# Four transfers instead of one for the reload of the residual, with a signal each, in a four-layer transformer kernel

## The chip, the cores and the metric

The kernel runs on one core of a Trainium2 chip, as one launch. The metric is the device time of that core in microseconds, the median of several runs; lower is better. In the traces PE is TensorE (matmuls and transposes), PEld its weight loads, DVE VectorE, ACT ScalarE, POOL GpSimd and SP SyncE, which in this kernel only issues transfers between memory and SBUF.

## The reference, cut to what matters

The input x has shape (32, 64, 256), that is N = 2048 rows of D = 256 numbers, and goes through four layers, each of a "cond" part and an "ffn" part, with a residual sum around each layer:

```
x = x + L0_ffn(L0_cond(x, cond), ...)      # ffn: mixture of 8 experts, top 2, capacity 320 rows per expert
x = x + L1_ffn(L1_cond(x, cond), ...)      # cond: 4 gated experts and a shared one
x = x + L2_ffn(L2_cond(x, ...), ...)       # ffn: 8 experts, each takes its 512 best rows
x = x + L3_ffn(L3_cond(x, cond, ...), ...) # cond: norm, attention, MLP in hyperbolic form
```

The ffn parts of layers 0 and 2 scatter-add their experts' outputs to rows of the result. L3_cond begins with a layer norm over the 256 numbers of each row:

```
m = x.mean(-1); v = ((x - m) ** 2).mean(-1)
xn = layer_norm(logmap0(x));  xm = expmap0(xn * (1 + sc_msa) + sh_msa);  q = plin(xm, w_q, b_q); ...
```

## The kernel before, in words

The residual lives in SBUF as `st.res`, 128 partitions x 16 tiles x 256 numbers (2 MB); tile t holds rows 128 t to 128 t + 127. The 2048 rows are also spoken of as four blocks of 512 rows, NB = 4, four tiles (TPB = 4) each. `st.cT` is the same data turned, with the 256 numbers in two groups (KC = 2) on the partitions and the rows along the free axis.

The program is a row of phases. Each phase opens a `Block`, in which every engine gets its own instruction list; at the end of a block all engines meet, and only then does the next phase begin. At the end of a layer `layer_end` (lines 59 to 75) adds one more block, in which GpSimd clears the layer's semaphores; semaphores made by `of_pool_dma` are not cleared.

The expert phase `routed_moe_phase` (lines 529 to 730) runs twice, as e0 at the end of layer 0 and as e3 at the end of layer 2. Before it, the dispatch phase has written the residual to the DRAM tensor `token_sums` (`sums` in the code, line 449). In the phase, GpSimd gathers each expert's rows, TensorE multiplies, VectorE scales the results (line 700), and GpSimd adds them to `token_sums` by indirect transfers (line 597), counted in `y_out`. When all are in, SP brings `token_sums` back into `st.res` in one transfer (line 575) and waits for it (line 576).

What follows differs:

- After e0 come `layer_end` and `turn_phase` "t1" (lines 128 to 155): for c in 0, 1 and b in 0 to 3 TensorE turns four tiles (line 138), group g = 4c + b; VectorE copies the even groups (line 145) and ScalarE the odd ones (line 153) from PSUM to `st.cT`. Then the block ends, and l1_cond begins with SP's weight transfers (line 1119), of which the first writes into `st.res` again.
- After e3 come `layer_end` and `l3_cond` (from line 2189). The work of its engines follows an order written out by hand in `l3_order()`. It begins with the statistics of tiles 0 to 7 (line 2617), then the norm's lengths, logarithm and variance for these eight tiles together (lines 2622 to 2648), and `norm` of tiles 0 to 7 (`stretch` at line 2655, then line 2667). Tiles 0 to 3 use the first chunk of the modulation `mod`, tiles 4 to 7 the second. TensorE turns tiles 0 and 1 after norms 2 and 3 (line 2328); its first product with `w_qkv` (line 2342) waits for three weight and three bias transfers at once (`qkv_in` of 96). The result is read by line 2682, which also needs the norm's last factor (lines 1906 to 1908). Statistics of tiles 8 to 15 come in the middle of this first round.
- SP in `l3_cond` issues, in this order: modulation chunks 0 and 1 (two transfers of 512 KB each, line 2273), then w_q, b_q, w_k, b_k, w_v, b_v (lines 2286 and 2289), then chunk 2 once four norms are done, chunk 3 once eight are, and then w_o, gates, w_f1, w_f2 and the rest.

`turn_phase` runs once more, as "t0" at the start of the program, with its rows loaded by the setup phase, which waits for them.

Of the kernel before, what the change touches and what calls it, by code (L numbers as in the profile page):

```python
# [14 lines left out]
P = 128  # L15
# [71 lines left out]
def setup_phase(nc, sem, st, x, cond):  # L87

    loaded, const0, const1 = sem("setup_loaded"), sem("setup_const0"), sem("setup_const1")
    turned, kept = sem("setup_turned"), sem("setup_kept")  # L90
    with nc.sbuf_tensor("cond_rows", [B, D], F32) as cond_rows, \
            nc.psum_tensor("cond_ps", [P, KC, B], F32) as cond_ps, nc.Block() as block:

        @block.sync
        def _(sp):
            sp.dma_start(cond_rows[:, :], cond).then_inc(loaded, 16)
            sp.dma_start(st.res[:, :, :], x.rearrange("(t a) s d -> (a s) t d", a=2)).then_inc(st.res_loaded, 16)
            sp.wait_ge(st.res_loaded, 16)

        @block.gpsimd  # L100
        def _(pool):
            pool.memset(st.ident[:, :], 0.0).then_inc(const0, 1)
            pool.memset(st.tri[:, :], 1.0).then_inc(const0, 1)
            pool.memset(st.ones[:, :], 1.0).then_inc(const0, 1)
            pool.wait_ge(const0, 3)
            pool.affine_select(out=st.ident[:, :], in_=st.ident[:, :], compare_op=ALU.not_equal, fill=1.0,
                               base=0, pattern=[[-1, P]], channel_multiplier=1).then_inc(const1, 1)

            pool.affine_select(out=st.tri[:, :], in_=st.tri[:, :], compare_op=ALU.is_ge, fill=0.0,
                               base=0, pattern=[[1, P]], channel_multiplier=-1).then_inc(const1, 1)  # L110

        @block.tensor
        def _(pe):
            pe.wait_ge(loaded, 16)
            pe.wait_ge(const1, 2)
            for c in range(KC):
                last = pe.transpose(cond_ps[:, c, :], cond_rows[:, c * P:(c + 1) * P], st.ident[0:B, 0:B])
            last.then_inc(turned, 1)

        @block.vector  # L120
        def _(dve):
            dve.wait_ge(turned, 1)
            dve.tensor_copy(st.condT[:, :, :], cond_ps[:, :, :]).then_inc(kept, 1)
            dve.wait_ge(kept, 1)

def turn_phase(nc, sem, st, tag, src, dst):

    turned, kept = sem(tag + "_turned"), sem(tag + "_kept")  # L130
    with nc.psum_tensor(tag + "_ps", [P, 8, 4, P], F32) as ps, nc.Block() as block:

        @block.tensor
        def _(pe):
            for g in range(KC * NB):
                c, b = g // NB, g % NB
                for j in range(TPB):
                    last = pe.transpose(ps[:, g, j, :], src[:, b * TPB + j, c * P:(c + 1) * P], st.ident[:, :])
                last.then_inc(turned, 1)

        @block.vector
        def _(dve):
            for g in range(0, KC * NB, 2):
                dve.wait_ge(turned, g + 1)
                dve.tensor_copy(dst[:, g // NB, (g % NB) * BLK:(g % NB + 1) * BLK],
                                ps[:, g, :, :].rearrange("p a b -> p (a b)")).then_inc(kept, 1)
            dve.wait_ge(kept, KC * NB)

        @block.scalar
        def _(act):  # L150
            for g in range(1, KC * NB, 2):
                act.wait_ge(turned, g + 1)
                act.activation(dst[:, g // NB, (g % NB) * BLK:(g % NB + 1) * BLK],
                               ps[:, g, :, :].rearrange("p a b -> p (a b)"), ACT.Copy).then_inc(kept, 1)
            act.wait_ge(kept, KC * NB)
# [370 lines left out]
            link(dve.tensor_tensor(st.slot_row[:, :, :], got[:, :, :, 1], row[:, :, :], ALU.add))  # L526


def routed_moe_phase(nc, sem, st, tag, rows, sums, slots, W1, b1, W2, func, spares, later_weights=None):

    tiles = [(a, min(P, slots - a)) for a in range(0, slots, P)]
    J = len(tiles)
    names = ("b_in b_turned b_kept w1_hi w2_hi w1_split w2_split x_turned x_hi x_ready up_done act_done h_ready "
             "y_done scaled res_in").split()
    b_in, b_turned, b_kept, w1_hi, w2_hi, w1_split, w2_split, x_turned, x_hi, x_ready, up_done, act_done, h_ready, \
        y_done, scaled, res_in = (sem(f"{tag}_{x}") for x in names)
    w1_in, w2_in = ([sem(f"{tag}_{x}_in{i}") for i in range(2)] for x in ("w1", "w2"))
    y_out = sem.of_pool_dma(tag + "_y_out")
    gathered = [sem.of_pool_dma(f"{tag}_gathered{i}") for i in range(3 * J)]
# [1 line left out]
    with ExitStack() as mem:  # L541
# [17 lines left out]
        @block.sync  # L559
        def _(sp):  # L560
            for e in range(E8):
                if e >= 2:
                    sp.wait_ge(w1_split, 2 * (e - 1))
                sp.dma_start(w1_raw[e % 2], W1[e].rearrange("(c p) f -> p c f", p=P)).then_inc(w1_in[e % 2], 16)
                if e == 0:
                    sp.dma_start(st.b1rows[:, :], b1.rearrange("e (c p) -> (e c) p", p=P)).then_inc(b_in, 16)
                if e >= 2:
                    sp.wait_ge(w2_split, 2 * (e - 1))
                sp.dma_start(w2_raw[e % 2], W2[e].rearrange("(c p) d -> p c d", p=P)).then_inc(w2_in[e % 2], 16)
                if e == 1 and rounding:  # L570
                    rounding.load(sp)
            if rounding:
                rounding.store(sp)
            sp.wait_ge(y_out, 16 * E8 * J)
            sp.dma_start(st.res[:, :, :], sums[0:N, :].rearrange("(t p) d -> p t d", p=P)).then_inc(res_in, 16)
            sp.wait_ge(res_in, 16)

        @block.gpsimd
        def _(pool):
# [1606 lines left out]
    yield from moved(range(NT + HALF, 2 * NT), False)  # L2186


def l3_cond(nc, sem, st, x, dst, w, ada_rows):

    QKV_PARTS = lambda t: [(0, 512), (512, 768)] if t < HALF else [(0, 256), (256, 512), (512, 768)]
    qkv_before = lambda t: 2 * t if t <= HALF else 2 * HALF + 3 * (t - HALF)
# [4 lines left out]
    with ExitStack() as mem:  # L2197
# [412 lines left out]
        def _(dve):  # L2610
            link = Chain(dve, chain)
            mean, var = mv[:, :, 0], mv[:, :, 1]

            def stats(m):
                if m >= NT:
                    dve.wait_ge(moved, m - NT + 1)
                dve.bn_stats(six[:, m % NT, :], (x if m < NT else dst)[:, m % NT, :]).then_inc(stats_done, 1)
# [459 lines left out]
def adaln_ffn_4_layers(nc, a, out):  # L3077

    with ExitStack() as stack:
        sem = Sems(nc)  # L3080
        st = State(nc, stack, sem)
        w = lambda prefix, *names: [a[prefix + n] for n in names]
        spare = st.cT2[:, :, :].rearrange("p c (t d) -> p (c t) d", d=D)
        rows = nc.dram_tensor("token_rows", (N + PADS, ROW), F32).ap()
        sums = nc.dram_tensor("token_sums", (N + PADS, D), F32).ap()

        ada_rows = nc.dram_tensor("modulation_rows", (B, ADA), F32).ap()
        kept_gu = nc.dram_tensor("rounded_gate_up", (P, GT * D), F32).ap()
        kept_dn = nc.dram_tensor("rounded_down", (P, KC * HID), F32).ap()

        setup_phase(nc, sem, st, a["x"], a["cond_1024"])

        turn_phase(nc, sem, st, "t0", st.res, st.cT)
        l0_cond_phase(nc, sem, st, st.cT, st.cT2, *w("L0_cond_", "W_q", "b_q", "W_kv", "b_kv", "no_op_k", "no_op_v", "W_proj", "b_proj"))
        l0_router_phase(nc, sem, st, st.cT2, *w("L0_ffn_", "router_w", "router_b"),
                        *w("L3_cond_", "w_ada", "b_ada"), ada_rows)
        bias2_phase(nc, sem, st, "b20", st.gates, st.res, *w("L0_ffn_", "b2"))
        dispatch_phase(nc, sem, st, "d0", st.cT2, rows, sums)
        routed_moe_phase(nc, sem, st, "e0", rows, sums, CAPACITY, *w("L0_ffn_", "w1", "b1", "w2"), ACT.Gelu, [st.cT, st.cT2],
                         [*w("L3_ffn_", "w_gate", "w_up", "w_down"), kept_gu, kept_dn])  # L3100
        sem.layer_end()

        turn_phase(nc, sem, st, "t1", st.res, st.cT)
        l1_phases(nc, sem, st, a)
        sem.layer_end()

        l2_cond_phase(nc, sem, st, st.cT, st.cT2, *w("L2_cond_", "Wx", "Wh", "b"))
        l2_router_phase(nc, sem, st, st.cT2, *w("L2_ffn_", "Wr"))
        bias2_phase(nc, sem, st, "b23", st.gates, st.res, *w("L2_ffn_", "b2"), accT=st.cT)
        dispatch_phase(nc, sem, st, "d2", st.cT2, rows, sums)  # L3110
        routed_moe_phase(nc, sem, st, "e3", rows, sums, CHOSEN, *w("L2_ffn_", "W1", "b1", "W2"), ACT.Gelu, [st.cT, st.cT2])
        sem.layer_end()

        names = "w_q b_q w_k b_k w_v b_v w_o b_o w_f1 b_f1 w_f2 b_f2".split()
        l3_cond(nc, sem, st, st.res, spare, dict(zip(names, w("L3_cond_", *names))), ada_rows)
        sem.layer_end()
        l3_ffn_phases(nc, sem, st, spare, st.res, out, kept_gu, kept_dn)
        sem.stack.close()
        sem.kept.close()
# [18 lines left out]
```

## Time and profile before

| | |
|---|---|
| median of 3 runs | 2501.59 us (2500.58 to 2502.45) |
| the profiled execution's own time | 2501.92 us |
| its span in the profile | 2500.2 us |
| granted TensorE clock, mean over the span | 0.892 |
| busy: PE, DVE, ACT, POOL | 84%, 54%, 39%, 10% |
| moved by transfers | 146.01 MB, 58 GB/s over the span |

The page cuts the span in 40 slices of 62.5 us; most of them show PE at 8 or 9 tenths. The reloads lie at 298.4 us (fifth slice) and 1839.5 us (thirtieth slice). In both slices PE is less busy than in those before them.

### The profile page before, as it was taken

The numbers are of one execution on the slowest core, as the hardware profiler recorded it, in microseconds if no ns is written. First come the engines' busy times: TensorE is split into PE (matmuls) and PEld (weight loads), VectorE is DVE, ScalarE is ACT, GpSimd is POOL, SyncE is SP. The second block draws the span as 40 slices with busy tenths as digits, with TensorE's granted clock in tenths as the row PEclk, the third lists the DMA queues.
The fourth block names the chain that finished last, engine by engine and source line by source line (L and its number), as shares of the span: only waits on it lengthen the run. The fifth ranks groups of instructions, "written<-read, shape, count | busy, mean of one in ns | idle before, by whom it ended". The sixth has DMA issues, their size and how long they took to land. (4 is left out here: it accounts for less than half of the span.)

```text
span 2500.2 us, 34348 instructions
## 1 busy us (share of the span) xinstructions
PE 2107.1 (84%) x13371; PEld 1693.4 (68%) x13371; DVE 1353.5 (54%) x2579; ACT 985.5 (39%) x1954; POOL 244.1 (10%) x207
## 2 busy tenths in 40 slices
PE   6788689999799999999999883789946777785786
PEld 5477668888687888888888673479934554554554
DVE  2589555777575444444343214456546446454885
ACT  2143255555253444444444220235423344454222
POOL 1144200000000000000000002047710000000000
PEclk7799889999899999999999995689976857897998
DMA  2375221233113121111100000265363001000000
GB/s 77 99 230 159 61 69 58 79 102 101 35 34 78 42 51 34 27 42 34 34 1 1 11 3 0 86 193 131 67 145 93 2 18 34 18 18 35 1 9 26
DMA packets 111492, 146.01 MB, mean 58 GB/s; under 512 B 6661, under 2 KB 94660, under 8 KB 111077
## 3 DMA queue, kind: packets, MB, share of 16 engines
q1 hardware_dynamic: 101220, 129.99, 17.3%
q0 software_dynamic: 10112, 13.85, 3.1%
q8 instruction: 106, 1.74, 0.3%
q14 instruction: 54, 0.43, 0.1%
HBM read 121.83 MB, written 21.99 MB: 58 GB/s over the span
## 5 line engine op out<-in xcount | busy, mean ns | idle before, releaser
L1598 DVE TENSOR_TENSOR m_h_lo<-m_hf,m_h_hi 128x512 fp32r<-128x512 f32 x256 | 172.1, 690 | 359.1 <-ACT m_hf L1573 357.2
L1570 ACT ACTIVATE m_h_hi<-m_h_ps,m_bT 128x512 fp32r<-128x512 f32 x256 | 177.0, 691 | 367.6 <-PE m_h_ps L394 348.0
L1573 ACT ACTIVATE m_hf<-m_h_ps,m_bT 128x512 f32<-128x512 f32 x256 | 175.0, 684 | 0.0
L597 POOL DMA_INDIRECT token_sums<-e_y,slot_row x56 | 145.7, 2602 | 159.4 <-DVE e_y L700 147.2
L662 ACT ACTIVATE e_h_hi<-e_h_ps,e_b1T 128x320 fp32r<-128x320 f32 (+1 forms) x128 | 78.0, 609 | 168.3 <-PE e_h_ps L394 102.2
L1310 DVE TENSOR_TENSOR c_h_lo<-c_hf,c_h_hi 128x512 fp32r<-128x512 f32 x120 | 82.3, 687 | 74.8 <-ACT c_hf L1269 73.7
L716 DVE TENSOR_TENSOR e_h_lo<-e_hf,e_h_hi 128x320 fp32r<-128x320 f32 (+1 forms) x128 | 74.1, 589 | 77.5 <-issue 44.4
L1837 POOL MEMSET n_bias<- 128x256 f32 x1 | 0.3, 312 | 1083.5 <-POOLq L59 1083.5
L1266 ACT ACTIVATE c_h_hi<-c_h_ps,c_b 128x512 fp32r<-128x512 f32 x88 | 62.2, 707 | 109.3 <-PE c_h_ps L394 108.8
L394 PE MATMUL m_y_ps<-m_h_hi,l_w_1hi 128*128 128x512 f32 x256 | 100.3, 392 | 3.5 <-issue 3.5
L394 PE MATMUL m_h_ps<-m_x_hi,l_w_0hi 128*128 128x512 f32 x256 | 100.6, 393 | 0.4 <-ACT m_b2T L1563 0.4
L394 PE MATMUL m_y_ps<-m_h_hi,l_w_0hi 128*128 128x512 f32 x256 | 99.7, 389 | 1.4 <-ACT m_gT L1584 1.4
L394 PE MATMUL m_y_ps<-m_h_hi,l_w_1lo 128*128 128x512 f32 x256 | 100.3, 392 | 0.0
L394 PE MATMUL m_h_ps<-m_x_hi,l_w_0lo 128*128 128x512 f32 x256 | 100.3, 392 | 0.0
L394 PE MATMUL m_h_ps<-m_x_lo,l_w_0hi 128*128 128x512 f32 x256 | 100.3, 392 | 0.0
L394 PE MATMUL m_y_ps<-m_h_lo,l_w_1hi 128*128 128x512 f32 x256 | 100.2, 391 | 0.0
L394 PE MATMUL m_y_ps<-m_h_hi,l_w_0lo 128*128 128x512 f32 x256 | 99.6, 389 | 0.0
L394 PE MATMUL m_y_ps<-m_h_lo,l_w_0hi 128*128 128x512 f32 x256 | 99.6, 389 | 0.0
L394 PE MATMUL m_h_ps<-m_x_hi,l_w_1hi 128*128 128x512 f32 x256 | 99.6, 389 | 0.0
L394 PE MATMUL m_h_ps<-m_x_lo,l_w_1hi 128*128 128x512 f32 x256 | 99.6, 389 | 0.0
L394 PE MATMUL m_h_ps<-m_x_hi,l_w_1lo 128*128 128x512 f32 x256 | 99.6, 389 | 0.0
L2342 PE MATMUL l_ps<-l_w_qkv,l_qkv_T 128*128 128x256 f32 (+1 forms) x160 | 64.7, 548 | 28.5 <-ACT l_qkv_T L2493 19.2
(644 smaller groups left out, 5607.7 us busy)
## 6 DMA issues: line engine op xcount, KB each, us to landing
cT<-in_L_ffn_W_dram SPq DMA_DIRECT2D x30, 1024.0 KB, 5.3
res<-in_L_cond_ew_dram SPq DMA_DIRECT2D x22, 1024.0 KB, 5.3
cT<-in_L_ffn_w_dram SPq DMA_DIRECT2D x16, 1024.0 KB, 7.0
res<-gates_rows SPq DMA_DIRECT2D x8, 1024.0 KB, 15.0
l_mod<-modulation_rows SPq DMA_DIRECT2D x16, 512.0 KB, 6.6
token_rows<-d_tok SPq DMA_DIRECT2D x2, 2112.0 KB, 9.9
token_sums<-res SPq DMA_DIRECT2D x2, 2048.0 KB, 7.6
res<-token_sums SPq DMA_DIRECT2D x2, 2048.0 KB, 8.4
```

The costliest lines, as they stand in the source:

```text
L394: ins = pe.matmul(out, lhs[a], rhs[b], start=(first and i == 0), stop=(last and i == 2))
L597: pool.indirect_dma_start(out=sums, out_offset=bass.IndirectOffsetOnAxis(ap=st.slot_row[0:r, e, j:j + 1], axis=0), in_=y[0:r, e % 2, j, :] ...
L662: act.activation(hs[0][:, f, :], h_ps[:, f % HB, 0:slots], func, bias=b1T[:, n:n + 1])
L716: dve.tensor_tensor(hs[1][:, f, :], hf[:, f % HB, :], hs[0][:, f, :].bitcast(F32), ALU.subtract).then_inc(h_ready, 1)
L1266: act.activation(hs[0][:, f, :], h_ps[:, f % HB, :], ACT.Gelu_apprx_tanh, bias=b[:, f:f + 1])
L1310: dve.tensor_tensor(hs[1][:, f, :], hf[:, f % HB, :], hs[0][:, f, :].bitcast(F32), ALU.subtract).then_inc(h_ready, 1)
L1570: act.activation(hs[0][:, f, :], h_ps[:, f % HB, :], ACT.Relu, bias=bT[:, at:at + 1])
L1573: act.activation(hf[:, f % HB, :], h_ps[:, f % HB, :], ACT.Relu, bias=bT[:, at:at + 1]).then_inc(act_done, 1)
L1598: dve.tensor_tensor(hs[1][:, f, :], hf[:, f % HB, :], hs[0][:, f, :].bitcast(F32), ALU.subtract).then_inc(h_ready, 1)
L1837: pool.memset(bias[:, :], 0.0).then_inc(bias_set, 1)
L2342: last = pe.matmul(ps[:, qkv_bank(t, p), 0:z - a], qkv_T[:, t % 2, k, :], w_qkv[:, k, a:z], start=(k == 0), stop=(k == KC - 1))
```

## The change

- Line 575's one transfer of 2 MB becomes four of 512 KB, one for each block of 512 rows. Each has a semaphore of its own, four for the first reload and four for the second. The wait at line 576 goes.
- The semaphores are made by `of_pool_dma`, so `layer_end` does not clear them.
- `turn_phase` takes the list of semaphores: TensorE waits for block b's ahead of the four transposes of (c = 0, b). For "t0" none are given, and it stays as it was.
- In `l3_cond` VectorE waits for block m/4's semaphore ahead of the statistics of tiles 0, 4, 8 and 12. All later readers of `st.res` there come behind the statistics.

```
-def turn_phase(nc, sem, st, tag, src, dst):
+def turn_phase(nc, sem, st, tag, src, dst, src_in=None):
...
             for g in range(KC * NB):
                 c, b = g // NB, g % NB
+                if src_in is not None and c == 0:
+                    pe.wait_ge(src_in[b], 16)
                 for j in range(TPB):
...
             sp.wait_ge(y_out, 16 * E8 * J)
-            sp.dma_start(st.res[:, :, :], sums[0:N, :].rearrange("(t p) d -> p t d", p=P)).then_inc(res_in, 16)
-            sp.wait_ge(res_in, 16)
+            for b in range(NB):
+                sp.dma_start(st.res[:, b * TPB:(b + 1) * TPB, :],
+                             sums[b * BLK:(b + 1) * BLK, :].rearrange("(t p) d -> p t d", p=P)).then_inc(res_in[b], 16)
...
             def stats(m):
+                if m < NT and m % TPB == 0:
+                    dve.wait_ge(x_in[m // TPB], 16)
                 if m >= NT:
                     dve.wait_ge(moved, m - NT + 1)
...
+        res_in = [[sem.of_pool_dma(f"res_in{i}_{b}") for b in range(NB)] for i in range(2)]
...
-        turn_phase(nc, sem, st, "t1", st.res, st.cT)
+        turn_phase(nc, sem, st, "t1", st.res, st.cT, res_in[0])
...
-        l3_cond(nc, sem, st, st.res, spare, dict(zip(names, w("L3_cond_", *names))), ada_rows)
+        l3_cond(nc, sem, st, st.res, res_in[1], spare, dict(zip(names, w("L3_cond_", *names))), ada_rows)
```

## Rows read from the trace of the kernel before

**Rows 1.** The page: the 40 slices of PE busy and of granted clock.

```profile
PE   6788689999799999999999883789946777785786
...
PEclk7799889999899999999999995689976857897998
```

**Rows 2.** Timeline, first reload: start, length (us), engine, line, out<-in, [idle before <-releaser].

```profile
298.40 0.37 SPq L575 DMA_DIRECT2D res<-token_sums  x1
...
308.16 5.23 PE L138 MATMUL t_ps<-ident,res 128*128 128x128 f32 x32 [18.00 <-PEq L59]
309.28 0.69 DVE L145 COPY cT<-t_ps 128x512 f32<-128x512 f32 x1 [17.82 <-PE t_ps L138]
310.13 0.60 ACT L153 ACTIVATE cT<-t_ps 128x512 f32<-128x512 f32 x1 [27.47 <-PE t_ps L138]
...
312.99 0.69 DVE L145 COPY cT<-t_ps 128x512 f32<-128x512 f32 x1 [0.18 <-PE t_ps L138]
313.43 0.60 ACT L153 ACTIVATE cT<-t_ps 128x512 f32<-128x512 f32 x1 [0.28 <-PE t_ps L138]
314.48 0.38 SPq L1119 DMA_DIRECT2D res<-in_L_cond_sw_dram  x1
```

**Rows 3.** Transfers by line: count, KB each, median us from issue to landing.

```profile
cT<-in_L_ffn_W_dram SPq DMA_DIRECT2D x30, 1024.0 KB, 5.3
...
res<-token_sums SPq DMA_DIRECT2D x2, 2048.0 KB, 8.4
...
l_wkv<-in_L_cond_W_kv_dram SPq DMA_DIRECT2D x1, 512.0 KB, 3.8
```

**Rows 4.** Windows, first reload: PE, PEld, DVE, ACT, POOL, clock, DMA share, GB/s.

```profile
305.00:306.00 1.00, 0.00 (x0) 0.00 (x0) 0.00 (x0) 0.00 (x0) 0.00 (x0) 0.50 0.98 308
306.00:307.00 1.00, 0.00 (x0) 0.00 (x0) 0.00 (x0) 0.00 (x0) 0.00 (x0) 0.50 0.09 29
...
308.10:311.40 3.30, 3.24 (x16) 3.27 (x17) 1.10 (x2) 0.60 (x1) 0.00 (x0) 0.51 0.00 0
311.40:314.50 3.10, 1.99 (x18) 1.75 (x16) 1.67 (x3) 1.80 (x4) 0.01 (x1) 1.00 0.00 0
```

**Rows 5.** Timeline, second reload and start of l3_cond.

```profile
1839.49 0.37 SPq L575 DMA_DIRECT2D res<-token_sums  x1
1848.87 2.62 SPq L2273 DMA_DIRECT2D l_mod<-modulation_rows  x4
...
1848.92 2.71 DVE L2617 BATCH_NORM_STATS2 l_six<-res 128x6 f32<-128x256 f32 x8 [18.36 <-PEq L59]
...
1857.82 0.88 DVE L2655 SCALAR_TENSOR_TENSOR l_xn<-res,l_mv,l_mod 128x256 f32<-128x256 f32 x2
...
1861.68 0.48 DVE L2655 SCALAR_TENSOR_TENSOR l_xn<-res,l_mv,l_mod 128x256 f32<-128x256 f32 x1 [0.62 <-DMA l_mod<-modulation_rows]
...
1864.42 4.51 PE L2342 MATMUL l_ps<-l_w_qkv,l_qkv_T 128*128 128x512 f32 x8 [3.60 <-DMA l_b_qkv<-in_L_cond_b_v_dram]
...
1867.17 0.17 DVE L1908 SCALAR_TENSOR_TENSOR l_fac<-l_nv,l_fac 128x8 f32<-128x8 f32 x1
...
1868.20 1.25 DVE L2682 SCALAR_TENSOR_TENSOR l_wide<-l_ps,l_fac,l_b_qkv 128x512 f32<-128x512 f32 x2 [0.86 <-PE l_ps L2342]
```

**Rows 6.** Windows, second reload and start of l3_cond, columns as in rows 4.

```profile
1847.00:1848.00 1.00, 0.00 (x0) 0.00 (x0) 0.00 (x0) 0.00 (x0) 0.00 (x0) 0.50 0.09 31
...
1850.00:1851.00 1.00, 0.00 (x0) 0.00 (x0) 1.00 (x5) 0.17 (x1) 0.00 (x0) 0.50 0.57 182
...
1856.00:1857.00 1.00, 0.00 (x0) 0.00 (x0) 0.66 (x4) 0.20 (x1) 0.00 (x0) 0.50 1.07 211
...
1862.00:1863.00 1.00, 0.00 (x0) 0.00 (x0) 0.90 (x3) 0.40 (x2) 0.00 (x0) 0.50 1.07 377
```

**Rows 7.** Timeline, SP in l3_cond: a short issue and one held up.

```profile
1855.25 0.47 SPq L2289 DMA_DIRECT2D l_b_qkv<-in_L_cond_b_v_dram  x1
...
1873.65 7.34 SPq L2289 DMA_DIRECT2D l_b_f<-in_L_cond_b_f_dram  x1
```

More of the change, by code:

```diff
@@ L526, in _, with routed_moe_phase @@
             link(dve.tensor_tensor(st.slot_row[:, :, :], got[:, :, :, 1], row[:, :, :], ALU.add))
-def routed_moe_phase(nc, sem, st, tag, rows, sums, slots, W1, b1, W2, func, spares, later_weights=None):
+def routed_moe_phase(nc, sem, st, tag, rows, sums, slots, W1, b1, W2, func, spares, res_in, later_weights=None):
     tiles = [(a, min(P, slots - a)) for a in range(0, slots, P)]
@@ L533, in routed_moe_phase @@
     names = ("b_in b_turned b_kept w1_hi w2_hi w1_split w2_split x_turned x_hi x_ready up_done act_done h_ready "
-             "y_done scaled res_in").split()
+             "y_done scaled").split()
     b_in, b_turned, b_kept, w1_hi, w2_hi, w1_split, w2_split, x_turned, x_hi, x_ready, up_done, act_done, h_ready, \
-        y_done, scaled, res_in = (sem(f"{tag}_{x}") for x in names)
+        y_done, scaled = (sem(f"{tag}_{x}") for x in names)
     w1_in, w2_in = ([sem(f"{tag}_{x}_in{i}") for i in range(2)] for x in ("w1", "w2"))
@@ L2186, in l3_order, with l3_cond @@
     yield from moved(range(NT + HALF, 2 * NT), False)
-def l3_cond(nc, sem, st, x, dst, w, ada_rows):
+def l3_cond(nc, sem, st, x, x_in, dst, w, ada_rows):
     QKV_PARTS = lambda t: [(0, 512), (512, 768)] if t < HALF else [(0, 256), (256, 512), (512, 768)]
@@ L3098, in adaln_ffn_4_layers @@
         dispatch_phase(nc, sem, st, "d0", st.cT2, rows, sums)
-        routed_moe_phase(nc, sem, st, "e0", rows, sums, CAPACITY, *w("L0_ffn_", "w1", "b1", "w2"), ACT.Gelu, [st.cT, st.cT2],
+        routed_moe_phase(nc, sem, st, "e0", rows, sums, CAPACITY, *w("L0_ffn_", "w1", "b1", "w2"), ACT.Gelu, [st.cT, st.cT2], res_in[0],
                          [*w("L3_ffn_", "w_gate", "w_up", "w_down"), kept_gu, kept_dn])
         sem.layer_end()
-        turn_phase(nc, sem, st, "t1", st.res, st.cT)
+        turn_phase(nc, sem, st, "t1", st.res, st.cT, res_in[0])
         l1_phases(nc, sem, st, a)
@@ L3110, in adaln_ffn_4_layers @@
         dispatch_phase(nc, sem, st, "d2", st.cT2, rows, sums)
-        routed_moe_phase(nc, sem, st, "e3", rows, sums, CHOSEN, *w("L2_ffn_", "W1", "b1", "W2"), ACT.Gelu, [st.cT, st.cT2])
+        routed_moe_phase(nc, sem, st, "e3", rows, sums, CHOSEN, *w("L2_ffn_", "W1", "b1", "W2"), ACT.Gelu, [st.cT, st.cT2], res_in[1])
         sem.layer_end()
         names = "w_q b_q w_k b_k w_v b_v w_o b_o w_f1 b_f1 w_f2 b_f2".split()
-        l3_cond(nc, sem, st, st.res, spare, dict(zip(names, w("L3_cond_", *names))), ada_rows)
+        l3_cond(nc, sem, st, st.res, res_in[1], spare, dict(zip(names, w("L3_cond_", *names))), ada_rows)
         sem.layer_end()
```

## The prediction

> **What bounds the kernel now.** I read the page first [rows 1]: TensorE is busy at 8 or 9 tenths through most of the span, so a change away from it is worth nothing except where it stands idle. The two slices with the reloads are such places. The timelines and windows around them show how long nobody works. At the first [rows 2, 4] SP issues at 298.40, the transfer takes 8.4 us [rows 3], so it lands at 306.80, and TensorE's first transpose is at 308.16: 1.36 us for SP to leave its block, the semaphore block and the entry of the next. The data had stopped moving shortly after 306.0 (DMA share 0.98, then 0.09). The 32 transposes take 5.23 us, with the copies right behind, and the next phase starts at 314.48. At the second [rows 5, 6] the issue is at 1839.49, the landing by the same 8.4 at 1847.89, and the next phase starts at 1848.87. All engines are idle until then. So both reloads lie whole on the path that sets the end, and any microsecond saved there is saved at the end, unless a later wait takes it.
>
> **The first reload, step by step.** SP now issues four transfers. The short issues of this queue take 0.37 to 0.47 us [rows 2, 7] and four issues in a row took 2.62 us [rows 5], so SP is done 1.5 to 2.6 us after 298.40. It then goes through the block ends, about 1.36 us, and TensorE stands in front of its first wait at 301.3 to 302.4. When does block 0 land? 512 KB took 3.8 us, 1 MB 5.3 and 2 MB 8.4 [rows 3]: about 3.0 us per MB more and a start of some 2.3. One after another on one queue without gaps they land at about 302.2, 303.7, 305.3 and 306.8. The block ends are then hidden under the first transfer; without that cover they would cost their 1.36 us again. For the three extra completions I add 0.2 us, bounds 0 (the long window of rows 6 shows no gap between transfers) and 1.0: last landing 307.0.
>
> TensorE turns blocks 0 to 2 of c = 0 meanwhile. After the last landing remain 4 transposes of block 3 and 16 of c = 1, five groups of four. A group takes 0.85 us at the low clock (309.28 to 310.13) and 0.44 at the high one (312.99 to 313.43) [rows 2]; the granted clock was 0.51 until 311.4 and 1.00 after [rows 4], 1.2 and 2.4 GHz. In the kernel before, it rose after 3.3 us of unbroken transposes. Afterwards TensorE works in pieces of 0.85 us with 0.7 us of idleness between them until 307, so the clock may be up at once (five groups 2.2 us) or never within this phase (4.25). I take 3.5: like before, about 3.3 us low and then high. PE ends at 307.0 + 0.1 + 3.5 = 310.6, the last ScalarE copy and the block's end add the same 1.09 us as now (313.39 to 314.48), and the next phase starts at 311.7 instead of 314.5. **Gain 2.8 us**; bounds 1.0 (clock low throughout, 1.0 us of extra completions) and 4.3 (clock high at once, none).
>
> The Trainium skill, "TensorE: Matmul & The Clock Gate", Part 4: PE-mode transpose, says that transposes do not bring the clock up. By that rule the five groups would take 4.25 us and the gain would be 2.0; the trace speaks against it, since the clock rose to 1.00 with nothing but transposes running [rows 4].
>
> The four waits in TensorE's list stand only in c = 0; queued behind each are the later groups, and VectorE and ScalarE wait for those. The copies, 0.69 and 0.60 us each on two engines [rows 2], keep step and have done c = 0's first three before the end, so they stay one copy behind. l1_cond's weight transfer into st.res comes behind the block's end, as now; it and everything after move along with it.
>
> **The second reload.** Here two chains run. VectorE's: statistics of tiles 0 to 7 need only blocks 0 and 1, which land at about 1843.3 and 1844.8. Each four take 1.36 us (2.71 for eight), so they end at 1846.2 instead of 1851.63 [rows 5]: 5.4 us earlier. The statistics of tiles 8 to 15 wait for blocks that have landed 20 us before, at no cost. But the norms also need the modulation and TensorE the weights, and those come on the same queue behind the residual. Now tile 4's stretch at 1861.68 waits for chunk 1 of the modulation, and the first product at 1864.42 for the last bias. Between 1850.4 and that landing the transfer engines are full (share 0.57, then 1.07) [rows 6]. What can be gained there is the pause in which they carry nothing: the residual's data end at 1847.1 (0.09), the modulation's begin at 1850.4 (0.57 of the slice). SP would issue the modulation from 1839.49 + 2.0 + 1.0 = 1842.5 on, well ahead of 1847.1, so the queue goes straight on and everything behind arrives 3.3 us earlier: chunk 1 at 1858.4, the bias at 1861.1. The chain behind chunk 1 (to the factor at 1867.34) and the one behind the bias (to 1868.20) end within 0.9 us of each other and move equally. Less 0.2 for the completions and 0.1 for hand-over: **gain 3.0 us**. Upper bound 5.4 (VectorE's whole lead), lower bound 0. Most of VectorE's lead turns into a wait for chunk 0, then for chunk 1.
>
> **Sum.** 2.8 + 3.0 = 5.8 us. The profiled execution took 2501.92 us (span 2500.2), the median is 2501.59, 0.3 lower. 2501.9 - 5.8 = 2496.1 for such an execution, 2495.8 for the median. Elsewhere nothing is touched: four more waits in TensorE's and VectorE's lists and six more issues on SP, all counted above.
>
> **The rivals.**
> - **The queue or SP holds the modulation back.** A later bias issue took 7.34 us instead of 0.47 [rows 7], so SP can be stopped while many transfers are pending. With 2 MB pending and four chunks behind them it could be stopped here; if the modulation's data then begin one start (1.5 us, from issue at 1848.87 to data at 1850.4) after the residual's end, the second gain is 3.3 - 1.5 = 1.8 less 0.3, and with the low clock at the first reload (2.0) the sum is 3.5: 2498.1. For it: the held issue. Against: ten transfers in a row were issued here without such a stop. 21%.
> - **The block's end waits for SP's own transfers.** Then removing line 576 does nothing but shorten SP's last step, and the start is as late as now: 0 to 1 us of gain, 2501.1. Nothing in the trace shows a block left with a transfer pending, so it is open. 6%.
> - **The modulation is not queued behind the residual but shares the engines with it, and VectorE's chain sets the end.** Its lead of 5.4 us survives: 2.8 + 5.4 = 8.2, time 2493.4. Against: the share of 1.07 has no room for more. 7%.
> - **Slower: four transfers are served one by one, each with its own start.** Place: the queue between 298.4 and the last landing, and the same at the second. Four times 3.8 is 15.2 instead of 8.4 us, the last landing 6.8 later. First reload: 313.6 + 0.1 + 3.5 + 1.1 = 318.3, 3.8 us later; second: the modulation's data begin at 1853.9 (6.8 after 1847.1) instead of 1850.4, 3.5 later: sum 7.3, time 2508.9. It decides once the extra starts delay the last landing by over 2.9 us, about 1 us each. Against: ten transfers of 128 to 512 KB in a row kept the share at 1.0 [rows 5, 6]. 5%.
>
> The Trainium skill, "DMA: Bandwidth & Descriptors", Bandwidth, advises transfers of at least 1 MiB and speaks against cutting 2 MB in four. Its price is that of the last rival if nothing overlaps; rows 6 show small ones overlapping.
>
> **How the numbers follow.** The forecast has 61%. Its own range is 2493.9 to 2498.6: the two gains at (4.3, 3.4) and (1.0, 2.0). About a tenth of a percent, 2.5 us, is one free choice of the clock's rise at the two places; executions also scatter by 1 us. The whole range, 2493.2 to 2499.6, takes in the third rival and most of the first and leaves out the second, the slow one and some tails. 0.2%, about what a measurement of this kernel can tell from no change, is 5.0 us, so 2496.6. The forecast falls on the faster side in four of five cases: 0.49 + 0.07 = 0.56. Same: 0.12 + 0.21 + 0.06 = 0.39. Slower: 0.05.
>
> **What would show it.** Right: four issues of SP, landings about 1.5 us apart, the last within 0.5 of the old one; the turning's first transposes before the last landing; the phase start at line 1119 some 13.3 us after the issue instead of 16.1; no empty slice between the residual's and the modulation's data; line 2682 first at some 25.7 us after the issue instead of 28.7. Wrong: TensorE's first transpose after the last landing (second rival), landings 3 us apart or more (slow rival), a gap in the transfers with a long SP issue (first rival). If all these hold and the time is still off by over 2 us, a wait further down took the gain, most likely a clock that fell or rose elsewhere.

## The result, and the profile after

| | before | changed |
|---|---|---|
| median of 10 runs each | 2500.85 us (2497.80 to 2506.03) | 2492.35 us (2490.34 to 2495.29) |
| ratio, 95% interval | | 0.9967 [0.9958, 0.9976] |
| profiled execution, its span | 2501.92, 2500.2 us | 2495.29, 2493.6 us |
| mean granted clock of the profiled execution | 0.892 | 0.889 |

The changed kernel is 8.5 us faster in the medians (6.0 to 10.5 us by the interval), where 5.8 us was forecast; 2492.35 us lies 0.85 below the lower end of the range. The profiled pair is 6.6 us apart; the changed kernel's profiled execution was the slowest of its ten. Executions of one kernel differ by more than I had taken: 8 us between the fastest and slowest of the ten before, where the three runs shown ahead of the prediction spanned 1.9. Of all executions behind this document one was far slower than the rest, 2850.83 us in e12, and it is left out of e12's ratio.

The page of the changed kernel, the same slices as [rows 1]. The slices of the two reloads rise by one digit each (fifth 6 to 7, thirtieth 4 to 5), and two others move as well, so the reloads have to be read in time order:

```profile
PE   6788789999799999999999883879956777785786
```

The timeline of the changed kernel's first reload (SP and TensorE, then the last copy), which answers to [rows 2]:

```profile
298.50 2.02 SPq L578 DMA_DIRECT2D res<-token_sums  x4
...
302.56 1.11 PE L140 MATMUL t_ps<-ident,res 128*128 128x128 f32 x4 [12.24 <-DMA res<-token_sums]
304.06 1.12 PE L140 MATMUL t_ps<-ident,res 128*128 128x128 f32 x4 [0.39 <-DMA res<-token_sums]
305.57 1.11 PE L140 MATMUL t_ps<-ident,res 128*128 128x128 f32 x4 [0.39 <-DMA res<-token_sums]
306.97 4.53 PE L140 MATMUL t_ps<-ident,res 128*128 128x128 f32 x20 [0.29 <-DMA res<-token_sums]
...
311.54 0.60 ACT L155 ACTIVATE cT<-t_ps 128x512 f32<-128x512 f32 x1 [1.11 <-PE t_ps L140]
...
312.61 0.37 SPq L1122 DMA_DIRECT2D res<-in_L_cond_sw_dram  x1
```

TensorE's waits end on the transfers, 1.5 us apart, the last 8.47 us after the first issue. Over the six profiled executions with four transfers and TensorE waiting for them (the changed kernel, e1, e5, e6, e8, e9) this is 8.29 to 8.49 us, with one transfer 8.31 (e3): the cut into four costs the last landing some 0.1 us. After it, 20 transposes take 4.53 us instead of the 3.5 of the forecast. The reason is in the windows of the changed kernel (columns as in [rows 4]): the clock stayed at 0.50 through all the transposes, 1.2 GHz, and rose only once they were done.

```profile
302.50:311.50 9.00, 7.87 (x32) 6.28 (x32) 2.77 (x4) 1.79 (x3) 0.00 (x0) 0.50 0.46 146
311.50:312.60 1.10, 0.00 (x1) 0.00 (x0) 0.00 (x0) 0.60 (x1) 0.00 (x0) 0.92 0.00 0
```

From the first issue to the next phase it is 14.11 us; it was 16.08. The first place gave 2.0 us in this pair.

The timeline of the changed kernel's second reload, against [rows 5]:

```profile
1837.21 2.02 SPq L578 DMA_DIRECT2D res<-token_sums  x4
1841.10 2.62 SPq L2276 DMA_DIRECT2D l_mod<-modulation_rows  x4
...
1841.15 2.82 DVE L2622 BATCH_NORM_STATS2 l_six<-res 128x6 f32<-128x256 f32 x8 [12.89 <-PEq L59]
...
1847.22 2.44 SPq L2292 DMA_DIRECT2D l_b_qkv<-in_L_cond_b_v_dram  x1
...
1850.96 0.88 DVE L2660 SCALAR_TENSOR_TENSOR l_xn<-res,l_mv,l_mod 128x256 f32<-128x256 f32 x2 [0.84 <-DMA l_mod<-modulation_rows]
...
1855.59 0.48 DVE L2660 SCALAR_TENSOR_TENSOR l_xn<-res,l_mv,l_mod 128x256 f32<-128x256 f32 x1 [1.38 <-DMA l_mod<-modulation_rows]
...
1858.46 4.24 PE L2345 MATMUL l_ps<-l_w_qkv,l_qkv_T 128*128 128x512 f32 x8 [4.49 <-DMA l_b_qkv<-in_L_cond_b_v_dram]
...
1861.12 0.60 SPq L2289 DMA_DIRECT2D l_w_o<-in_L_cond_w_o_dram  x1
...
1861.97 1.25 DVE L2687 SCALAR_TENSOR_TENSOR l_wide<-l_ps,l_fac,l_b_qkv 128x512 f32<-128x512 f32 x2 [0.72 <-PE l_ps L2345]
```

The windows of the changed kernel there, against [rows 6]:

```profile
1844.00:1845.00 1.00, 0.00 (x0) 0.00 (x0) 0.93 (x10) 0.00 (x0) 0.00 (x0) 0.50 1.11 353
1845.00:1846.00 1.00, 0.00 (x0) 0.00 (x0) 0.62 (x5) 0.69 (x2) 0.00 (x0) 0.50 1.11 217
```

The engines go from the residual (353 GB/s) to the modulation (217 GB/s) with no gap, at a share of 1.11 on both sides. The statistics end 6.8 us after the issue (12.1 before), a lead of 5.4 us. Part of it is then spent in two waits for the modulation, 0.84 and 1.38 us, where the kernel before had one of 0.62: 1.6 us more waiting. The first product starts 21.25 us after the issue; it was 24.93. Its reader at line 2687 (2682 before) starts at 24.76 instead of 28.71: 3.95 us.

### The profile page after: what moved, and what is told of

Read it like the earlier page. It is cut to its first block and busy times, and to the rows that moved or that the text cites. A ratio compares the mean times of both kernels' runs of the same rounds, so it can differ in the third digit from the quotient of the medians.

```text
span 2493.6 us, 34352 instructions
## 1 busy us (share of the span) xinstructions
PE 2112.0 (85%) x13371; PEld 1695.6 (68%) x13371; DVE 1353.4 (54%) x2579; ACT 984.9 (39%) x1954; POOL 245.7 (10%) x207
```

## The experiments

Twelve runs followed: seven new kernels (e1 to e4, e6, e7, e12), the changed kernel twice more (e5, e8), and e1, e2 and e7 once more (e9, e10, e11). The columns "first" and "second" are read from one profiled execution each: "first" is from the first issue of the first reload to SP's first issue of the next phase, "second" from the first issue of the second reload to w_o's issue, which waits for the eighth norm. "At the places" is the sum of both against the means of the kernels that have the old code there (first 16.12 us: before, e2, e10; second 27.40: before, e1, e4, e9). The last column is the gain in time: one minus the run's ratio, the one given with its interval, times the median of before on that chip. It can differ from the plain difference of the medians, by up to 2 us (e8: 7.5 and 9.6).

| kernel | first, us | second, us | at the places, us | span, us | gain in time, us |
|---|---|---|---|---|---|
| before | 16.08 | 27.73 | | 2500.2 | |
| changed | 14.11 | 23.91 | 5.5 | 2493.6 | 8.3 |
| e1 first only | 13.36 | 27.34 | 2.8 | 2495.0 | 3.0 |
| e2 second only | 16.16 | 23.57 | 3.8 | 2493.0 | 2.7 |
| e3 one transfer, late wait | 15.40 | 26.41 | 1.7 | 2497.2 | 5.2 |
| e4 four transfers, early wait | 17.07 | 27.36 | -0.9 | 2502.2 | 0.0 |
| e5 changed, again | 14.08 | 23.80 | 5.6 | 2493.1 | 8.8 |
| e6 kept warm | 12.00 | 25.01 | 6.5 | 2491.3 | 8.0 |
| e7 rows first | 11.54 | 21.86 | 10.1 | 2486.4 | 15.0 |
| e8 changed, third | 13.93 | 23.76 | 5.8 | 2490.4 | 7.5 |
| e9 first only, again | 14.06 | 27.17 | 2.3 | 2495.9 | 4.0 |
| e10 second only, again | 16.13 | 23.88 | 3.5 | 2497.6 | 5.3 |
| e11 rows first, again | 11.72 | 21.78 | 10.0 | 2486.4 | 11.3 |
| e12 rows first, warm | 11.20 | 21.83 | 10.5 | 2490.9 | 15.5 |

Mostly the two lengths repeat within some tenths where the code of the place is the same. Where the first does not (13.36 against 14.1, 17.07 against 16.1) the clock came up at another moment. The second has one exception, e6: its code there is that of the changed kernel, but it took 25.01 us against 23.57 to 23.91; the wait for chunk 1 of the modulation ended 19.5 us after the issue instead of 18.4. The spans repeat within some microseconds only, and the intervals of the last column are 2 to 5 us to either side. Twelve of the thirteen gains in time are larger (e2 is not) than the gain at the places, and a line through zero fitted to all thirteen has a slope of 1.4. They are not thirteen independent values: the runs of one chip (e1 to e4, e5 to e7, e8 to e11) share one set of executions of the kernel before.

### e1, e2: each half alone

```
-        res_in = [[sem.of_pool_dma(f"res_in{i}_{b}") for b in range(NB)] for i in range(2)]
+        res_in = [[sem.of_pool_dma(f"res_in{i}_{b}") for b in range((NB, 1)[i])] for i in range(2)]   # e1; e2: (1, NB)
...
+            if len(res_in) == 1:
+                sp.dma_start(st.res[:, :, :], sums[0:N, :].rearrange("(t p) d -> p t d", p=P)).then_inc(res_in[0], 16)
+                sp.wait_ge(res_in[0], 16)
...
```

Otherwise the four transfers are issued as in the changed kernel. Also, e1 goes without the waits in l3_cond's stats, e2 with turn_phase called as before.

> Four transfers and per-block waits at the first reload alone; the second reload is as before. Theory A (both gains are local and add up; in the profiled pair the first was worth 2.0 us and the second 3.7): this run gains 2.0 us if the clock stays low through the turning and up to 4 if it comes up, over many executions about 3. Theory B (the gain of 8.5 us in the medians, 3 more than the two places show, comes from the clock of later stages, moved by the earlier start): this run gains over 4.5 us and the two halves do not add up to the whole.

Measured: 2496.10 us (11 runs) against 2499.92 (35 runs), ratio 0.9988 [0.9978, 0.9999]. In the profiled execution the clock did come up during the last 20 transposes. TensorE's rows in the timeline of e1:

```profile
305.50 1.12 PE L140 MATMUL t_ps<-ident,res 128*128 128x128 f32 x4 [12.16 <-DMA res<-token_sums]
...
309.93 3.25 PE L140 MATMUL t_ps<-ident,res 128*128 128x128 f32 x15 [0.30 <-DMA res<-token_sums]
```

The view ends at 313; all 20 took 3.79 us, against 4.53 in the changed kernel. The length is 13.36 us, 2.8 us below the 16.1 of e2 and the kernel before. That is the case of the forecast; the changed kernel's own execution, 14.11, had the clock low for longer.

> Four transfers and per-block waits at the second reload alone. Theory A: gains 3.7 us, and from the issue of the reload to the first read of the first qkv product 24.8 us instead of 28.7. Theory B: a gain over 5 us with the same local 3.7.

Measured: 2497.00 us (11 runs) against the same 2499.92, ratio 0.9989 [0.998, 0.9998]. The local length is 23.57, 3.8 us below the mean of the unchanged ones. Read by e1 and e2 alone, the halves give 0.23% together and the whole 0.33%, on other chips; the intervals are too wide to call that a difference, so it was repeated (e8 to e10).

### e3: hide the block ends, but bring one transfer

```
-            for b in range(NB):
-                sp.dma_start(st.res[:, b * TPB:(b + 1) * TPB, :],
-                             sums[b * BLK:(b + 1) * BLK, :].rearrange("(t p) d -> p t d", p=P)).then_inc(res_in[b], 16)
+            sp.dma_start(st.res[:, :, :], sums[0:N, :].rearrange("(t p) d -> p t d", p=P)).then_inc(res_in[0], 16)
...
+        res_in = [[sem.of_pool_dma(f"res_in{i}")] * NB for i in range(2)]
```

> One transfer of 2 MB as before at both places, but SP leaves its block at once, and TensorE and VectorE wait for the whole transfer where the changed kernel waits for blocks. It keeps the hiding of the block ends and the queueing of the modulation behind the residual, and leaves out the early blocks. If the block ends are the main part of the first gain: 1.3 us there. At the second reload the queue theory (the engines' pause of 3.3 us closes) says the whole 3.7 us stays, since the modulation lands as early; the theory that VectorE's lead sets the end says that only 1.0 us stays. Sum 5.0 by the queue theory, 2.3 by the other.

Measured: 2495.21 us (12 runs, from 2488.63 to 2501.07) against 2499.92, ratio 0.9979 [0.9968, 0.999]. Read by the time alone, this 4.7 us would have spoken for the queue theory (5.0); the places say otherwise, and this is the clearest case of a gain in time (2.5 to 8.0 us by the interval) beyond them (1.7). The first place gives 0.7 us instead of 1.3: TensorE starts its transposes 8.31 us after the issue, 1.4 us earlier than before, but with the clock low for longer they took 6.00 us, against 5.23. The second place gives 1.0 us, not 3.7. The timeline of e3 shows why:

```profile
1846.94 2.62 SPq L2274 DMA_DIRECT2D l_mod<-modulation_rows  x4
...
1851.68 2.71 DVE L2620 BATCH_NORM_STATS2 l_six<-res 128x6 f32<-128x256 f32 x8 [17.59 <-DMA res<-token_sums]
...
1860.57 0.88 DVE L2658 SCALAR_TENSOR_TENSOR l_xn<-res,l_mv,l_mod 128x256 f32<-128x256 f32 x2
...
1864.68 4.60 PE L2343 MATMUL l_ps<-l_w_qkv,l_qkv_T 128*128 128x512 f32 x8 [1.10 <-ACT l_qkv_T L2494]
...
1869.46 0.61 SPq L2287 DMA_DIRECT2D l_w_o<-in_L_cond_w_o_dram  x1
```

The modulation is queued early here too, but VectorE's statistics begin 8.6 us after the issue, and none of its stretches waits for the modulation afterwards; TensorE's first product now waits for ScalarE's turned tile, not for the bias. So the two chains are close to each other, within 3 us: close the engines' pause alone and VectorE's chain binds (1.0 us gained), bring the blocks early too and the queue binds (3.6). The queue theory as written, with nothing of VectorE in it, falls for this kernel. Of the second gain 2.6 us need the early blocks on top of the closed pause, though the queue sets its size. The early blocks without the closed pause were not run; in the kernel before, tile 4's stretch already waited 0.62 us for the modulation [rows 5], so they should bring nothing by themselves.

### e4: the price of cutting alone

```
                              sums[b * BLK:(b + 1) * BLK, :].rearrange("(t p) d -> p t d", p=P)).then_inc(res_in[b], 16)
+            for b in range(NB):
+                sp.wait_ge(res_in[b], 16)
```

and no waits in turn_phase or stats.

> Four transfers, but SP waits for all four before it leaves its block, at both places; nobody else waits. This is the price of cutting alone: if the transfers overlap as the trace of the changed kernel shows (landings 1.5 us apart, the last 8.3 us after the first issue), no change, within 0.5 us. If each pays a start of its own, slower by 2 us or more at each place.

Measured: 2500.45 us (11 runs) against 2499.92, ratio 1.0 [0.9991, 1.0009]. SP's rows in the timeline of e4:

```profile
1846.12 2.02 SPq L578 DMA_DIRECT2D res<-token_sums  x4
1855.66 2.62 SPq L2278 DMA_DIRECT2D l_mod<-modulation_rows  x4
```

The modulation's first issue comes 9.54 us after the reload's, where the one transfer had 9.33 to 9.38: 0.2 us for four transfers and four waits. The slow rival is ruled out. The Trainium skill, "DMA: Bandwidth & Descriptors", Bandwidth, asks for transfers of 1 MiB or more; here four of 512 KB in a row cost 0.2 us over one of 2 MB.

### e5: the whole again

> The changed kernel again, unaltered. The two halves alone gained 3.8 and 2.9 us in their medians (2496.10 and 2497.00 against 2499.92), some 6 together, but the whole had shown 8.5. Theory A (local gains that add up, the rest is scatter of the clock over the run): this run gains 5.5 to 6.5 us in the median, and locally 2.0 to 2.8 at the first reload and 3.5 to 3.8 at the second. Theory B (something beyond the halves): again over 8 us.

Measured: 2493.18 us (5 runs) against 2501.62 (17 runs), ratio 0.9965 [0.9952, 0.9979], 8.4 us in the medians. Locally 14.08 and 23.80: 2.0 and 3.6 us. So here, too, the medians show more than the places do, though 5.6 lies inside the interval of this run (5.3 to 12.0 us).

### e6: TensorE kept warm

```
                 if src_in is not None and c == 0:
+                    for _ in range(6 if b == 0 else 2):
+                        pe.transpose(ps[:, KC * NB - 1, 0, :], st.ident[:, :], st.ident[:, :])
                     pe.wait_ge(src_in[b], 16)
```

> The changed kernel with extra transposes of the identity into an unused part of PSUM ahead of the waits of the first reload's turning: six ahead of block 0, two ahead of blocks 1 to 3. Their results are never read. Theory: the clock stays low through the turning because TensorE works in pieces; if it works nearly without a pause from 301 to 307 us the clock is up at the last landing, and the last five groups take 2.2 us instead of 3.3 to 4.4: from the first issue to the next phase 11.9 to 12.5 us instead of 13.4 to 14.1. Rival: the clock does not depend on these, and the stretch stays at 13.4 to 14.1 or grows by 0.2 for the extra work.

Measured: first length 12.00 us, 2.1 us below the changed kernel. The timeline of e6:

```profile
302.99 1.51 PE L139 MATMUL t_ps<-ident 128*128 128x128 f32 x6 [11.65 <-PEq L59]
...
307.95 2.40 PE L142 MATMUL t_ps<-ident,res 128*128 128x128 f32 x20 [0.53 <-DMA res<-token_sums]
```

and its windows, with the clock up before the last landing:

```profile
304.00:305.00 1.00, 1.00 (x7) 1.00 (x6) 0.00 (x0) 0.00 (x0) 0.00 (x0) 0.50 1.10 347
305.00:306.00 1.00, 1.00 (x7) 1.00 (x6) 0.61 (x1) 0.00 (x0) 0.00 (x0) 0.60 1.10 346
306.00:307.00 1.00, 0.96 (x9) 0.73 (x8) 0.09 (x1) 0.60 (x1) 0.00 (x0) 1.00 1.09 346
```

The 20 transposes behind the last landing take 2.40 us against 4.53. What the changed kernel lacks at the first place is the clock. Whether it stays low because of the short pauses, as the theory had it, this run doesn't show (see e7). The Trainium skill, "TensorE: Matmul & The Clock Gate", Part 4: PE-mode transpose, says transposes do not raise it; here nothing but transposes ran from 303 to 307 and it rose to 1.00, so the trace disagrees. The median is 2493.09 us (12 runs), like e5's 2493.18 on the same chip: 2 us at one place are not enough to show against the scatter, and in e6's profiled execution the second place was 1.2 us longer (25.01).

### e7: turn block by block, and bring blocks 2 and 3 late

```
-                c, b = g // NB, g % NB
+                c, b = (g % KC, g // KC) if src_in is not None else (g // NB, g % NB)
...
-            for b in range(NB):
+            for b in range(NB if rounding else 2):
...
                 bias(b_qkv[:, i * D:(i + 1) * D], w["b_" + name], qkv_in)
+            for b in range(2, NB):
+                sp.dma_start(x[:, b * TPB:(b + 1) * TPB, :],
+                             sums[b * BLK:(b + 1) * BLK, :].rearrange("(t p) d -> p t d", p=P)).then_inc(x_in[b], 16)
```

The two copies of the turning take c and b in the same way. The second loop stands in l3_cond, behind the modulation's chunks 0 and 1 and the qkv weights; the expert phase e3 issues only blocks 0 and 1.

> Two further steps on the changed kernel. The turning goes block by block, both groups of columns of a block together, so that only 8 of 32 transposes stand behind the last landing. And at the second reload blocks 2 and 3 are issued by l3_cond behind the modulation and the qkv weights, ahead of which they need not be. If the first place is bound by the transposes behind the last landing: 12.0 us from first issue to next phase instead of 13.4 to 14.1 (with the clock low the four blocks take 1.7 us each against landings 1.5 apart). If the second is bound by the queue: all landings 3 us earlier, until VectorE's own chain binds, so a gain of 2.2 to 2.7 there; issue to w_o's issue 21.5 instead of 23.9. Sum 3.5 to 4.5 below the changed kernel. If VectorE's chain bound the second place already, only the first step gains.

Measured: 2487.19 us (6 runs) against 2501.62, ratio 0.994 [0.9921, 0.9959]; again in e11. Locally 11.54 and 21.86. The timeline of e7:

```profile
301.88 6.54 PE L140 MATMUL t_ps<-ident,res 128*128 128x128 f32 x32 [12.12 <-DMA res<-token_sums]
...
1843.51 4.59 SPq L2302 DMA_DIRECT2D res<-token_sums  x2
1846.70 0.88 DVE L2665 SCALAR_TENSOR_TENSOR l_xn<-res,l_mv,l_mod 128x256 f32<-128x256 f32 x2
...
1852.65 5.16 PE L2350 MATMUL l_ps<-l_w_qkv,l_qkv_T 128*128 128x512 f32 x8 [2.95 <-DMA l_b_qkv<-in_L_cond_b_v_dram]
```

At the first place TensorE is now busy from the first landing on, and when the last block lands some three groups of four are left (6.54 us for all eight, of which 1.96 behind 306.46, if the block lands 8.47 after the issue as in the changed kernel). The clock speaks against the theory of e6: TensorE transposed without a pause from 301.88, and the clock was still at 0.50 up to 306.5 and at 0.68 on average from there to the end. It came up about 5.8 us after the first transpose (6.1 in e11), where e6, e1 and the kernel before had it 2.8 to 3.2 us after the start of their last unbroken stretch, and e3 and the changed kernel 4.7. So pauses alone do not decide when it rises, and what does stays open. At the second the first product starts 18.9 us after the issue (21.25 in the changed kernel), and the stretches wait for nothing any more: VectorE's chain binds them, as expected, after 2 us.

### e8 to e11: whole, halves and the better kernel on one chip

> The changed kernel a third time, now on one chip with its two halves (the two looks so far, 8.2 and 8.5 us of gain, were on other chips than the halves, 2.6 and 3.3). Theory A (the local gains add, 6.1 us by the traces so far, and scatter of the clock did the rest): this gain is within 1.5 us of the sum of the next two runs. Theory B (the whole does something more): it exceeds their sum by 2 us or more.

Measured: 2492.12 us (9 runs) against 2501.71 (26 runs), ratio 0.997 [0.9958, 0.9981].

> First reload alone, beside the whole. Theory A: gain 2.0 to 3.5 us, 13.4 to 14.1 us from first issue to next phase. Theory B: no more than 2.6 here while the whole gains over 8.

Measured: 2497.78 us (12 runs), ratio 0.9984 [0.9975, 0.9992].

> Second reload alone, beside the whole. Theory A: gain 3.5 to 4.5 us, 23.6 to 23.9 us from first issue to w_o's issue. Theory B: no more than 3.5 here while the whole gains over 8.

Measured: 2495.95 us (10 runs), ratio 0.9979 [0.9969, 0.9989].

The ratios of the halves are worth 4.0 and 5.3 us of 2501.7, together 9.3, that of the whole 7.5. The difference of 1.8 is more than theory A's 1.5, but it has the other sign than theory B's, and is small beside the intervals. In the means of all executions, in which the expectation gave its own figures, the halves gain 3.7 and 4.7 and the whole 8.0: within 0.4. So the halves add up, as theory A has it, and theory B's extra in the whole alone is not seen. Both halves, like the whole, come out larger in time here than at their places (4.0 against 2.3, 5.3 against 3.5), which e1 (3.0 against 2.8) and e2 (2.7 against 3.8) had not shown.

> The kernel with block-by-block turning and late blocks 2 and 3 again, beside the changed kernel on one chip. From the traces it should be 4.4 us below the changed kernel: 11.5 us at the first reload against 14.1, and 21.9 at the second against 23.8. If its median of 2487.2 was chance, the two are within 2 us of each other.

Measured: 2489.03 us (5 runs), ratio 0.9955 [0.994, 0.997]; 3.1 us below e8 on the same chip, and locally 2.2 and 2.0 below it. The better kernel's medians lie below the changed kernel's on both chips where they ran together; the intervals overlap, so that e7 is better is shown at the places, and in the time only made likely.

### e12: both ideas at the first place

```
                 if src_in is not None and c == 0:
+                    for _ in range(6 if b == 0 else 3):
+                        pe.transpose(ps[:, KC * NB - 1, 0, :], st.ident[:, :], st.ident[:, :])
```

on top of e7.

> The kernel that turns block by block and brings blocks 2 and 3 late, with the extra transposes of the identity: six ahead of block 0, three ahead of the others. If the clock is what is left at the first reload: up before the last landing, the last eight transposes take 0.9 us instead of 1.7, and from first issue to next phase it is 10.7 to 11.1 us instead of 11.5 to 11.7. Rival: the extra work only stands in the way, 11.7 or more. In the median no difference that this scatter can show.

Measured: median 2488.96 us of six executions (2850.83 among them) against 2501.69 (11 runs), ratio 0.9938 [0.9923, 0.9954]; first length 11.20 us, between the two expectations. The last rows of TensorE in the timeline of e12:

```profile
307.93 0.49 PE L139 MATMUL t_ps<-ident 128*128 128x128 f32 x3
...
308.26 1.04 PE L142 MATMUL t_ps<-ident,res 128*128 128x128 f32 x8
```

The last eight transposes do take 1.04 us, but they start 9.06 us after the first issue instead of 8.5: the extra transposes and those of block 2 are still ahead of them. With only eight left behind the last landing, warmth buys 0.4 us and its work costs part of that.

## Why the prediction was right or wrong

- **Both reloads on the path, transfers 1.5 us apart, block ends hidden: right.** Predicted landings at 302.2 to 307.0 from an issue at 298.40; TensorE's groups began at 302.56, 304.06, 305.57 and 306.97 from one at 298.50. SP took 2.02 us for four issues (1.5 to 2.6 predicted), and the next phase began 3.89 us after the first (3.0), still ahead of what it waits for.
- **The price of three more transfers: about as taken.** 0.2 us were assumed; e4 shows 0.2 with its four waits, and against e3 the last landing is some 0.1 us later.
- **First gain 2.8 us: 2.2 us by the traces.** Mean of the five executions with the change 13.91 us, of the three without (before, e2, e10) 16.12. The mis-sized term is the turning behind the last landing: 3.5 us assumed, 4.53 measured in the changed kernel. In four of the five executions with the change the clock stayed low throughout, the bound that the prediction gave with 4.25 us; in e1 it rose as forecast and the gain was 2.8. e6 shows that the clock is the cause, by raising it: 2.40 us for the same transposes. (The lower bound of this gain, 1.0, should have read 1.2 by the prediction's own terms.)
- **Second gain 3.0 us: 3.6 us by the traces.** Unchanged 27.73, 27.34, 27.36, 27.17 (mean 27.40), changed 23.91, 23.57, 23.80, 23.76, 23.88 (mean 23.78). With the 25.01 of e6, which has the same code there, the mean is 23.99 and the gain 3.4. The mechanism is as forecast: the pause closes, and VectorE waits for the two chunks. But only 1.6 us of its lead of 5.4 turn into waiting, not most of it. Two terms were off: the 0.3 us deducted for completions and hand-over do not show, and by the windows the modulation ran at its full share at once (1.11, against 0.57 in its first slice before), an estimated 0.3 more. What the prediction did not see is how close VectorE's chain is behind: e3 shows that without the early blocks only 1.0 us of this is had.
- **Sum at the two places: 5.8 us forecast, 5.8 measured** (2.2 + 3.6; 5.6 with e6's second place). That it agrees is luck: the first gain is 0.6 less than forecast and the second 0.6 more.
- **The time: 5.8 us forecast, 8.5, 8.4 and 9.6 us in three pairs of medians; by the ratios 8.3, 8.8 and 7.5.** The step that failed is the one called the sum: "Elsewhere nothing is touched", taken to mean that nothing elsewhere changes. The runs showed some 2.5 us more than the two places hold. Each pair by itself says little: 5.8 lies just outside the interval of the first (6.0 to 10.5) and inside those of e5 (5.3 to 12.0) and e8 (4.8 to 10.5). The three ratios weighted by their intervals give an estimate of 8.1 us, give or take 1.6, against 5.6 to 5.8 at the places.
- **Where these 2.5 us come from stays open.** They come from outside the two places, where the code is the same, and the table shows that they do not belong to the changed kernel alone: most experiments gain more in time than at their places. One sign points to TensorE's clock, which the prediction named as the likeliest cause if the time were off by over 2 us. On one chip the mean granted clock was 0.8903 over 26 executions of the kernel before and 0.8922 over the nine of e8; as time at the low level (twice the missing share of the span) that is 548 and 537 us, 11 less, where the shorter places explain at most 5.8. Between executions of the kernel before on that chip a microsecond less at the low level goes with 0.2 us less of span (correlation 0.85), so the other 5 us would account for about 1 of the 2.5. Over the twelve runs, too, the gain beyond the places goes with the drop in low-level time beyond them (correlation 0.80, 0.23 us for each microsecond). These are correlations and not a test.
- **The traces show no stage that holds the rest.** Outside the two places (span less both lengths) there are 2456.4 and 2457.8 us (before, e4) against 2455.6, 2455.2 and 2452.7 (changed three times), but e10 and e12, which have new code, have 2457.6 and 2457.9. The stretch ahead of the first reload, which no edit reaches, varies from 297.7 to 302.5 us, the one between the places from 1523.6 to 1528.9 and the one behind w_o's issue from 626.5 to 633.0, and none of them sets the old code apart from the new (the first pair has 298.4, 1525.0 and 633.0 before, 298.5, 1524.6 and 632.5 changed). No experiment was made that moves the start of the later stages by itself.
- **The range was too narrow.** It was built from the two places and 1 us of scatter, from three runs that happened to lie within 2 us of each other; 2492.35 lies 0.85 us below it. In ten the kernel before spread over 8.2 us, in 35 over 9.
- **The rivals.** SP was indeed held at the last bias (2.44 us instead of 0.47), but after the modulation had been queued, and the modulation's data followed the residual's without a gap, so the first rival cost nothing there. The block's end does not wait for SP's own transfers: the next phase began 3.89 us after the first issue, with half of the residual or more still on its way (the last landed at 8.47), and in e6 TensorE was in its phase after 3.53. The third rival, the modulation beside the residual, is not seen (landings on time, both at a share of 1.11); its total of 8.2 us is near the measured one, but by another way than its own: the second place gave 3.6, not 5.4. Transfers served one by one: excluded by e4.

## What to carry to other kernels

When a phase begins with a reload, let the consumer wait for its own part and leave the block with the transfers in flight; order the parts, and the work on them, so that little stands behind the last landing, and send ahead only what is needed first (e7, 4 us more at the two places). Before crediting a lead to one chain, look for the second chain within a few microseconds of it: here the closed pause alone gives 1.0 us of 3.6 (e3), and the early blocks alone, by the waits of the kernel before, nothing (not run). A gain of 0.2% needs the scatter of many executions, not of three, before a range is set around it.

## What the runs showed that was not expected

- TensorE's clock came up late and not at the same moment. Behind pieces of work with short pauses (1.1 us of transposes, up to 0.39 us idle, three times over) it stayed low through 20 unbroken transposes in four of five executions, where the same transposes with fillers between them had it at 1.00 before 307 us (e6); until the turning ended this cost 2.1 us. But in e7 and e11, without any pause, it took about 6 us, so what decides the moment was not found.
- Four transfers of 512 KB behind one another carry as much as one of 2 MB (353 GB/s at a share of 1.11 in a late slice of the changed kernel; 350 at 1.10 from 1845 to 1846 in the kernel before), and another kind of transfer behind them starts without a gap.
- The time of this kernel varies by 0.3% between executions of the same program on one chip, and goes with its mean granted clock. Gains made at two places came out larger in the whole, by a fitted factor of 1.4 with wide intervals, for a reason not found.
